# One core: attention value products of two slots at once, reciprocals as a bank fill, and query products two head groups to a bank

## The reference

```
n1 = layernorm(x)
q, k, v = n1 @ wq + bq, ctx @ wk + bk, ctx @ wv + bv
s = (q k^T / sqrt(32)) * mask;  s = -1e9 where s == 0
a = softmax(s) @ v                       # per head
x = x + a @ wo + bo
n2 = layernorm(x)
x = x + real(ifft(fft(n2) @ W)) + bias   # W complex, 512 x 512
```

## Time and profile before

| | |
|---|---|
| median of three runs | 458.8 us |
| span of the profiled execution | 457.1 us |
| PE busy | 442.1 us (97%) |
| DVE busy | 398.0 us (87%) |
| ACT busy | 372.6 us (82%) |
| POOL busy | 359.6 us (79%) |
| chain that ended last: PE | 79% |
| chain that ended last: DVE | 10% |

### The profile page before, as it was taken

How to read it: one execution, slowest core, us unless ns; L and a number is a source line. 1 busy time by engine, 2 the same in 40 slices (tenths; PEclk the granted TensorE clock), 3 DMA queues, 4 the chain that set the end, 5 groups by cost and what they waited for, 6 DMA issues and landing times.

```text
span 457.1 us, 11172 instructions
## 1 busy us (share of the span) xinstructions
PE 442.1 (97%) x3510; PEld 293.3 (64%) x3510; DVE 398.0 (87%) x630; ACT 372.6 (82%) x1434; POOL 359.6 (79%) x540
## 2 busy tenths in 40 slices
PE   6989898999999999999999999999999999999997
PEld 5777686777666666666666666666666666555444
DVE  3797699899999999999999999999999898999443
ACT  3358597789999999898989898989989888899720
POOL 6588744795889899998989898869899685976663
PEclk9999998999999999999999999999999999999999
DMA  8996752332445454545555445445433334330344
GB/s 288 392 368 182 236 195 71 97 86 71 90 92 142 122 147 115 152 110 143 128 134 138 116 107 148 91 114 147 115 96 70 97 74 98 70 93 13 82 104 126
DMA packets 85287, 60.16 MB, mean 132 GB/s; under 512 B 40141, under 2 KB 72813, under 8 KB 84718
## 3 DMA queue, kind: packets, MB, share of 16 engines
q1 hardware_dynamic: 84508, 59.29, 47.3%
q10 hardware_dynamic: 722, 0.17, 0.2%
HBM read 29.33 MB, written 8.39 MB: 83 GB/s over the span
## 4 chain that ended last, share of the span: by engine, by line
PE 79%; DVE 10%; issue 5%; ACT 3%; DMA 1%; ACTq 0%; POOL 0%; DVEq 0%
PE bank L438 32%; PE bank L525 17%; PE bank L582 10%; PE bank L599 6%; PE scores L570 5%; PE bank L443 4%; DVE zs L867 3%; PE bank L595 3%; DVE zs L860 1%; ACT zs L688 1%; DMA bqb<-in_bq 1%; PE scores L443 1%; DVE cn L883 1%; ACT pt L697 1%; DVE x L845 1%
## 5 line engine op out<-in xcount | busy, mean ns | idle before, releaser
L688 ACT ACTIVATE zs<-zs,nbias 128x128 f32<-128x128 f32 x512 | 199.6, 397 | 8.2 <-POOL nbias L1093 7.9
L688 ACT ACTIVATION_READ_ACCUMULATOR zs<-zs,nbias 128x1 f32 x512 | 99.4, 194 | 0.0
L867 DVE SCALAR_TENSOR_TENSOR zs<-zs 128x1024 f32<-128x1024 f32 x64 | 81.3, 1270 | 0.2
L872 DVE TENSOR_REDUCE nmin<-zs 128x8 f32<-128x1024 f32 x64 | 78.1, 1220 | 2.2
L860 DVE TENSOR_TENSOR zs<-scores,ms 128x1024 f32<-128x1024 f32 x64 | 78.0, 1218 | 0.3 <-issue 0.3
L525 PE MATMUL bank<-xth,wqh 128*128 128x256 f16 x256 | 70.9, 277 | 4.0 <-DVE kl L810 2.0
L697 ACT COPY pt<-bank 128x512 f32<-128x512 f32 x128 | 68.4, 586 | 6.7 <-PE bank L582 6.3
L525 PE MATMUL bank<-xtl,wqh 128*128 128x256 f16 x256 | 70.4, 275 | 0.0
L525 PE MATMUL bank<-xth,wql 128*128 128x256 f16 x256 | 70.4, 275 | 0.0
L582 PE MATMUL bank<-ident,zs 128*128 128x128 f32 x512 | 67.5, 275 | 0.7 <-ACT zs L688 0.7
L1053 POOL TENSOR_TENSOR xs<-xs,bob 128x512 f32<-128x512 f32 (+1 forms) x41 | 42.4, 1036 | 24.5 <-DVE zs L867 24.5
(11 more groups left out here) (118 smaller groups left out, 960.1 us busy)
## 6 DMA issues: line engine op xcount, KB each, us to landing
xs<-in_x SPq DMA_DIRECT2D x16, 512.0 KB, 4.2
xtr<-in_xt SPq DMA_DIRECT2D x16, 512.0 KB, 4.4
out<-x SPq DMA_DIRECT2D x31, 256.0 KB, 2.6
qs<-qh SPq DMA_DIRECT2D x120, 64.0 KB
lp<-in_lparts SPq DMA_DIRECT2D x4, 1024.0 KB, 9.0
qs<-ql SPq DMA_DIRECT2D x60, 64.0 KB
ms<-in_mask SPq DMA_DIRECT2D x16, 128.0 KB, 2.6
wqs<-in_wq SPq DMA_DIRECT2D x2, 512.0 KB, 6.8
```

Of the source, the lines that this page charges most:

```text
L688: last = act.activation(z, z, ACT.Exp, bias=nbias[:, s % 4, i:i + 1], scale=-NEG, accum_out=zsum[:, s % 4, i:i + 1])
L867: dve.scalar_tensor_tensor(out=z, in0=z, scalar=0.0, in1=z, op0=ALU.is_equal, op1=ALU.subtract).then_inc(eq_done, 1)
L872: dve.tensor_reduce(nmin[:, s % 4, :], zs[:, s % NZ].rearrange("p t h k -> p (t h) k"), AX.X, ALU.min).then_inc(mn_done, 1)
```

## The change

Slots are taken in pairs m = (2m, 2m+1) for everything behind the exponentials.

- PV for slots 2m and 2m+1 is done at once, as the **first** item of PE in slot 2m+4: eight products that fill the whole bank CX.
- The four transposes of both slots' spread reciprocals are a new fill `R`, late in slot 2m+4, in a G bank. `lo(R)` on DVE only frees the bank, once ACT has copied it.
- Query products of two head groups are one fill `QQ` (24 matmuls into 512 columns), late in odd slots from 7 on (and in slots 2, 4, 5, 6). The mean and deviation rows are a late fill `ST` of their own in slots with r = 0.
- `rec`, `cn`, `ch`, `cl`, reciprocal and spread are one operation for a pair, in odd slots, with twice the columns and one buffer; `qh` and `ql` of a QQ are one operation each.

The core of the diff:

```diff
-    queries = {2: [(2, 0), (2, 1)], 3: [(2, 2)], 4: [(2, 3), (3, 0)], 5: [(3, 1)], 6: [(3, 2), (3, 3)]}
+    queries = {2: (2, 0), 4: (2, 1), 5: (3, 0), 6: (3, 1)}
...
-        late = [("Q",) + f for f in queries.get(v, [divmod(v + 9, 4)]) if f[0] < NC]
+        late = []
+        if v % 2 == 0 and 0 <= v - 4 < NS:
+            late.append(("R", (v - 4) // 2))
+        if v % 4 == 0 and 3 <= v // 4 + 2 < NC:
+            late.append(("ST", v // 4 + 2))
+        if v in queries:
+            late.append(("QQ",) + queries[v])
+        elif v >= 7 and v % 2 == 1 and (v + 9) // 4 < NC:
+            late.append(("QQ", (v + 9) // 4, (v + 9) % 4 // 2))
...
         items = []
+        if v % 2 == 0 and 0 <= v - 4 < NS:
+            items += [("PV", (v - 4) // 2)]
         if 0 <= v - 2 < NS:
             items += [("PT", v - 2, 0), ("PT", v - 2, 1)]
         items += [("G", n) for n in mids]
         if 0 <= v + 1 < NS:
             items += [("S", v + 1, 0), ("S", v + 1, 1)]
-        if 0 <= v - 3 < NS:
-            items += [("PV", v - 3)]
         items += [("G", n) for n in lates]
...
+                elif kind == "QQ":
+
+                    pe.wait_ge(p_l1, c)
+                    for i in range(2):
+                        g = slice(256 * f + 128 * i, 256 * f + 128 * i + 128)
+                        mm = []
+                        for k in range(4):
+                            mm += [(wqh[:, k, g], xth[:, c % 2, k]), (wql[:, k, g], xth[:, c % 2, k]),
+                                   (wqh[:, k, g], xtl[:, c % 2, k])]
+                        last = full_mm(o[:, 256 * i:256 * i + 256], mm)
+                elif kind == "R":
+                    pe.wait_ge(p_rz, c + 1)
+                    for i in range(2):
+                        for t in range(2):
+                            a = 256 * i + 128 * t
+                            last = pe.transpose(o[:, a:a + 128], rzb[:, i, 4 * t:4 * t + 4, :], ident[:])
...
+            def weigh(m):
+                c, h = divmod(m, 2)
                 b = c // (NC // NB)
-                pe.wait_ge(pt_copied, 2 * s + 2)
-                if s >= 1:
-                    pe.wait_ge(cn_done, s)
+                pe.wait_ge(pt_copied, 4 * m + 4)
+                if m >= 1:
+                    pe.wait_ge(cn_done, m)
...
+                for i in range(2):
+                    for j in range(4):
+                        n = 32 * (8 * h + 4 * i + j)
+                        last = pe.matmul(CX[32 * j:32 * j + 32, 256 * i:256 * i + 256], vs[:, b, n:n + 32],
+                                         pt[:, i, j, :], start=True, stop=True)
...
+            def copy_rec(m):
+                n = at["R", m]
+                act.wait_ge(g_done, n + 1)
+                if m >= 1:
+                    act.wait_ge(cn_done, m)
+                act.copy(rec[:], G[n % 3][:].rearrange("p (i n) -> p i n", i=2)).then_inc(rc_done, 1)
...
-                if 0 <= v - 4 < NS:
-                    copy_rec(v - 4)
+                if v % 2 == 1 and 0 <= v - 5 < NS:
+                    copy_rec((v - 5) // 2)
...
+                elif kind == "R":
+                    dve.wait_ge(rc_done, c + 1)
...
-                elif kind == "ST":
+                elif kind in ("ST", "R"):
                     dve.engine_nop().then_inc(g_free, 1)
                     return
...
+            def ctx_norm(m):
+                dve.wait_ge(rc_done, m + 1)
+                if m >= 1:
+                    dve.wait_ge(p_cl, m)
+                dve.tensor_tensor(cn[:], CX[:].rearrange("p (i n) -> p i n", i=2), rec[:], ALU.mult).then_inc(cn_done, 1)
...
-                if v <= VP and 0 <= v - 3 < NS:
-                    spread(v - 3)
+                if v == VP:
+                    spread(0)
...
-                if v >= VP and 0 <= v - 2 < NS:
-                    spread(v - 2)
+                if v > VP and v % 2 == 1 and 0 <= v - 3 < NS:
+                    spread((v - 3) // 2)
```

More of the change, by code:

```diff
@@ L254, in build, with last_query @@
         for n, f in enumerate(fills):
-            if f[0] in ("Q", "U", "M", "K", "W1", "Z"):
+            if f[0] in ("Q", "QQ", "U", "M", "K", "W1", "Z"):
                 hi_count[n] = len(hi_count) + 1
+        def last_query(c):
+            return at["Q", c, 3] if c < 2 else at["QQ", c, 1]
         def tile_of(c, t):
@@ L334, in stack_q @@
             def stack_q(c):
-                sp.wait_ge(g_free, at["Q", c, 3] + 1)
+                sp.wait_ge(g_free, last_query(c) + 1)
                 if c >= 2:
@@ L345, in turn_x1n @@
                 if c == NC - 1:
-                    sp.wait_ge(g_done, at["Q", c, 3] + 1)
+                    sp.wait_ge(g_done, last_query(c) + 1)
                     sp.wait_ge(h2_done, n + 1)
@@ L524, in fill @@
                     for i, (a, b) in enumerate(mm):
[L525 to L531, removed]
+                        pe.matmul(o[:, 0:256], a, b, start=(i == 0), stop=False)
+                    pe.wait_ge(wz_lo, f // 2 + 1)
+                    pe.wait_ge(st_done, c + 1)
+                    last = pe.matmul(o[:, 0:256], wz[:, g], srow[:, c], start=False, stop=True)
+                elif kind == "QQ":
[13 more added lines that the diff above has]
+                            last = pe.transpose(o[:, a:a + 128], rzb[:, i, 4 * t:4 * t + 4, :], ident[:])
                 elif kind == "WO":
                     pe.wait_ge(o_lo, 2)
-                    pe.wait_ge(ch_done, 4 * c + 4)
-                    pe.wait_ge(p_cl, 4 * c + 4)
+                    pe.wait_ge(ch_done, 2 * c + 2)
+                    pe.wait_ge(p_cl, 2 * c + 2)
                     g = slice(128 * f, 128 * f + 128)
@@ L583, in turn @@
                 last.then_inc(pt_done, 1)
-            def weigh(s):
-                c, g = divmod(s, 4)
+            def weigh(m):
+                c, h = divmod(m, 2)
                 b = c // (NC // NB)
-                pe.wait_ge(pt_copied, 2 * s + 2)
-                if s >= 1:
-                    pe.wait_ge(cn_done, s)
+                pe.wait_ge(pt_copied, 4 * m + 4)
+                if m >= 1:
+                    pe.wait_ge(cn_done, m)
                 else:
                     pe.wait_ge(g_free, at["V", 0] + 1)
[L593 to L600, removed]
+                for i in range(2):
[3 more added lines that the diff above has]
+                                         pt[:, i, j, :], start=True, stop=True)
                 last.then_inc(pv_done, 1)
@@ L655, in hi @@
                 elif kind == "Q":
-                    if f == 2 and 3 <= c + 1 < NC:
-                        stat_copy(src, c + 1).then_inc(st_done, 1)
+                    last = act.copy(qh[:, c % 2, f, :], src[:, 0:256])
+                elif kind == "QQ":
                     if f == 0 and c == 2:
@@ L661, in hi @@
                         act.wait_ge(d_q[c % 2], stacked(c - 2))
-                    last = act.copy(qh[:, c % 2, f, :], src[:, 0:256])
+                    last = act.copy(qh[:, c % 2, 2 * f:2 * f + 2, :], src[:].rearrange("p (g n) -> p g n", g=2))
                 last.then_inc(g_hi, 1)
@@ L671, in split_hi @@
                 if c >= 2:
[L672 removed]
+                    act.wait_ge(g_done, last_query(c - 2) + 1)
                 act.copy(xth[:, c % 2], xtr[:, c % NT]).then_inc(h1_done, 1)
@@ L695, in copy_pt, with ctx_hi @@
                 if f == 0 and s >= 2:
-                    act.wait_ge(pv_done, s - 1)
+                    act.wait_ge(pv_done, s // 2)
                 act.copy(pt[:, s % 2, 2 * f:2 * f + 2, :], PB[f][:]).then_inc(pt_copied, 1)
[L699 to L706, removed]
+            def copy_rec(m):
[4 more added lines that the diff above has]
+                act.copy(rec[:], G[n % 3][:].rearrange("p (i n) -> p i n", i=2)).then_inc(rc_done, 1)
+            def ctx_hi(m):
+                c, h = divmod(m, 2)
+                act.wait_ge(cn_done, m + 1)
+                if h == 0 and c >= 2:
                     act.wait_ge(g_done, at["WO", c - 2, 1] + 1)
-                act.copy(ch[:, c % 2, g, :], cn[:, s % 2, :]).then_inc(ch_done, 1)
+                act.copy(ch[:, c % 2, 2 * h:2 * h + 2, :], cn[:]).then_inc(ch_done, 1)
             act.dma_start(bkc[:], bk).then_inc(d_b, 16)
@@ L763, in _ @@
                     exps(v - 1, 1)
-                if 0 <= v - 4 < NS:
-                    ctx_hi(v - 4)
+                if v % 2 == 1 and 0 <= v - 5 < NS:
+                    ctx_hi((v - 5) // 2)
                 if 0 <= v - 9 < 4:
@@ L833, in lo @@
                     last = dve.tensor_tensor(ql[:, c % 2, f, :], src[:, 0:256], qh[:, c % 2, f, :], ALU.subtract)
+                elif kind == "QQ":
+                    g = slice(2 * f, 2 * f + 2)
+                    last = dve.tensor_tensor(ql[:, c % 2, g, :], src[:].rearrange("p (g n) -> p g n", g=2),
+                                             qh[:, c % 2, g, :], ALU.subtract)
                 elif kind == "WO":
@@ L873, in least, with recip @@
```

(29 more changed lines are left out.)

## The result

The changed kernel takes 487.49 us (median of four runs, 486.98 to 487.75) against 458.81 before (458.41 to 458.97): ratio 1.0625, 95% interval 1.0611 to 1.064. It is **slower by 28.7 us**; forecast were 484 us and a range of 468 to 500. Its profiled execution spans 486.0 us.

A forecast was written before the change was run, and what follows sets the result against it. PE was taken to bound the kernel. The profile's 457.1 plus 14.0 (periods), 6.1 (start), 0 (end) and 5 (clock) gave 482.2; with the median 1.7 above the span, 484 us, range 468 to 500.

The forecast's parts named there:

- The added wait: In each slot with r = 1, PE's QQ waits 1.74 us for R's bank, freed behind DVE's minimum.
- the sum: Durations added from an even slot's head (r = 0): `ql` at 4.91, QQ at 11.25, period 25.89; also stepped through the start.
- The periods: Slots 12 to 54: eleven periods of four slots, each 1.27 us longer than 24.62, +14.0 us.
- The start: Slots 4 to 11: U of slot 5 and M of slot 9 wait for R's bank; +6.1 us, 2 to 9.
- my heads: Predicted start times of slots 6 to 12: 74.0, 82.3, 88.1, 95.5, 106.6, 111.3 and 118.4 us.
- The clock: PE falls to half clock once more in the start and in three of eleven periods; +5 us.
- The end: Slots 55 to 63 gain 0.6 us, the last WO comes 0.6 later in the tail; sum zero.
- (a): PE's clock falls in every period, 20.4 us in place of 5: 499 us; chance 0.13.
- (b): QQ's wait is about half, 0.9 us, period +0.4, start +4, no more clock falls: 467.5 us; chance 0.13.
- (c): Faster: R's bank is freed about when PE comes, periods gain 3.5 us, start nothing: 455 us; chance 0.09.
- (d): PV on PE costs 1.78 us a pair as before, +0.2 a pair: 486 us; chance within the main case's 0.62.
- the 1.1 to 1.2 that I gave as a sign: Sign that the forecast is right: PE's PV of eight products takes 1.1 to 1.2 us.

The follow-up runs named there:

- the version with the extra operation ahead of the freeing: Changed kernel plus one idle 1.22 us DVE operation directly ahead of freeing R's bank in slots 13, 17, ... 53; 503.37 us.
- both edits: Changed kernel with R's bank freed right behind `cn` and the eight products moved behind the scores of slot 2m+3; 461.03 us.
- the early freeing alone: Changed kernel with DVE freeing R's bank right behind `cn` instead of behind the minimum; 463.71 us.

## Why the prediction was right

**The added wait, right in place and size.** From the first product of slot 28 (timeline: PT at 229.87, products 1.00 before it, 228.87) to QQ at 240.12 are 11.25 us; the sum said 11.25. That it is exact is luck: two terms missed by 0.11 in opposite directions.

```profile
233.67 0.69 DVE L862 TENSOR_TENSOR ql<-bank,qh 128x512 f16<-128x512 f32 x1
234.28 0.68 DVE L869 SCALAR_TENSOR_TENSOR x<-bank,xs 128x512 f32<-128x512 f32 x1
235.00 0.69 DVE L971 BATCH_NORM_STATS2 st<-x 128x6 f32<-128x512 f32 x1
...
235.83 1.23 DVE L890 TENSOR_TENSOR zs<-scores,ms 128x1024 f32<-128x1024 f32 x1
236.97 0.68 DVE L914 TENSOR_TENSOR cn<-bank,rec 128x512 f32<-128x512 f32 x1
237.57 1.22 DVE L897 SCALAR_TENSOR_TENSOR zs<-zs 128x1024 f32<-128x1024 f32 x1
238.82 1.22 DVE L902 TENSOR_REDUCE nmin<-zs 128x8 f32<-128x1024 f32 x1
```

These are DVE's rows of that stretch, to be read beside the earlier trace rows. `ql` starts 4.80 after the head, not 4.91: eight products in a row take 1.00 us, not 1.14. From `x` to the next mask product are 1.55, not 1.44: taking the reciprocal out saved nothing there, since the aggregate then waits for the statistics before it. `ql` and `cn` cost 0.61 and 0.60, as worked out from 256 columns. PE was ready 9.59 after the head (238.01 + 0.45), not 9.51, so it waited 1.66; the row's 1.50 counts from the modelled end of the last score matmul. The period is 26.02, 0.13 above the sum. That `ql` of the even slot hangs on `qh` held as well, but in slot 28 only by 0.2 us: DVE's own queue was nearly as late, which the sum did not work out.

**The periods, right; +16.8 for +14.0.** The nine periods from slot 16 to slot 52 are 0.16 longer than the sum, 1.4 of the 2.8 in all. Another 0.9 is the first: slot 12 to 16 lasts 27.49 against 25.32 before, since DVE comes out of the start late and ST waits 1.44 for it. The last 0.5 lies in slots 52 and 53: a whole wait, but only half of a period's gain on PE, where I took an eleventh whole period.

**The start, right in cause and too small: +10.8 for +6.1.** The step that was mis-sized is M in slot 9. Up to there my heads held within 0.9 us (PT of slot 7 at 83.01, said 82.3; of slot 9 at 96.03, said 95.5). Then the sum had M start at 101.8 (the head of slot 10 at 106.6, less 4.8 of PE's work). It started at 103.45 and ran at half clock, in the timeline of PE:

```profile
69.83 1.99 PE L454 MATMUL bank<-tb,lp 128*128 128x256 f32 x8 [3.22 <-DVEq L847]
...
103.45 3.78 PE L454 MATMUL bank<-tb,us 128*128 128x256 f32 x8 [3.78 <-DVEq L847]
```

Both are waits for R's bank, U in slot 5 and M in slot 9, as named. In slot 9 `lo(R)` stood behind `ml`, which waited 0.81 for `mh` and then took 1.22, where in the same slot of the kernel before it took 0.69 (97.92); why it took longer was not tried:

```profile
102.15 1.22 DVE L881 SCALAR_TENSOR_TENSOR ml<-mf,mh 128x512 f16<-128x512 f32 x1 [0.81 <-ACT mh L688]
```

The head of slot 12 came at 123.08, 4.7 later than the 118.4 of the sum. Of this 1.65 is M's late start: 0.5 from the head of slot 9, the rest from the wait for `mh` and the longer `ml`. Another 2.7 were lost by the half clock that began while PE waited for M (5.4 us of work at half rate).

**The clock, wrong for the periods.** I had let it fall in three of eleven periods; it fell in none, in a profiled execution with eleven idles of 1.5 us. It fell once in the start, as before, but stayed at half from about 102 to 108.9 us (the window from 108 to 109 has 0.57). PE idled in the first 1.4 us of this, so 2.7 us of work were lost there instead of 1.7: the term is 1.0 where I had 5. It hid, by luck, most of what the start, the periods and the end lacked; without it the sum would have been 479, still inside the range.

**The end, +1.8 for +0.6.** The pair's `cl` takes 1.16 where one slot's took 0.68, and the last WO fills stand behind it; how the rest divides was not tried.

**Rivals.** (a) did not come: no fall in any period. (b) and (c) needed `ql` earlier than the chain allows; it started within 0.11 of where the sum had it, and with `qh` out of the way DVE would have come only 0.2 earlier, so (c) had no ground in this slot. (d): PV was cheaper than before, 1.00 for eight products, and also than the 1.1 to 1.2 that I gave as a sign.

## What to carry to other kernels

In a rotation of buffers that is freed in order, count the fills between producer and waiter again after every edit of the list, and the work of the waiting engine between them: two merges, each of which alone left the period nearly as it was, made nine fills of eight, and one tenant's release came in the very slot that waits for it, behind 4 us of unrelated work. When an engine releases a buffer by an empty instruction, put that instruction where the buffer's last reader is known to be done, not where the list of evacuations happens to stand. And look at what hangs on a producer before moving work ahead of it: PV ahead of PT delayed everything behind PT by 1.00 us, and taking it away shortened the period by 1.19.

## What the runs showed of the hardware

**How long PE idles does not alone decide whether its clock falls.** In the kernel before, the clock fell with an idle of 1.60 us. In the changed kernel it did not fall with 3.22 us in slot 5 and did with 3.78 us in slot 9 (windows: PE busy, clock, DMA share, GB/s):

```profile
71.00:73.00 2.00, 2.00 (x21) 1.00 0.23 55
102.00:104.00 2.00, 0.55 (x1) 0.51 0.00 0
104.00:106.00 2.00, 2.00 (x6) 0.50 0.00 0
```

The list of work does not decide it either. Up to slot 12 the version with the extra operation ahead of the freeing is the changed kernel. Its U of slot 5 waited as long, and it ran at half clock (the window from 68 to 69 us has 0.74, the one from 69 to 70 has 0.50):

```profile
69.66 2.93 PE L456 MATMUL bank<-tb,lp 128*128 128x256 f32 x6 [3.21 <-DVEq L849]
```

In the periods of that version eleven waits of PE for the bank last 2.62 us each; after one of them its clock was half. The timeline shows it in the duration of the first matmul behind the wait, 0.39 for 0.28:

```profile
219.97 0.28 PE L456 MATMUL bank<-xth,wqh 128*128 128x256 f16 x1 [2.62 <-DVEq L849]
...
328.56 0.39 PE L456 MATMUL bank<-xth,wqh 128*128 128x256 f16 x1 [2.62 <-DVEq L849]
```

and the windows of that version the clock (same columns as above):

```profile
326.00:328.00 2.00, 0.00 (x0) 0.97 0.69 206
328.00:330.00 2.00, 1.45 (x7) 0.50 0.84 241
330.00:332.00 2.00, 2.00 (x15) 0.67 0.12 49
```

Two idles of the same length, 2.62 us, with and without a fall. What else decides was not tried.

**The falls set runs of one kernel apart.** With both edits the runs at a mean granted clock of 1.000 took 460.3 to 461.29 us, those at 0.996 took 462.34 and 462.85; with the early freeing alone it was 462.48 and 463.69 to 463.8. A mean of 0.996 is about what one stretch of 3.4 us at half leaves over such a span (1.7 of 462 us). Versions that differ by less than 1 to 2 us can be told apart only by runs of the same mean clock.

**A row of products 32 columns wide pays something at its ends.** Four took 0.57 us, eight 1.00, from the first start to the next instruction; and the group ahead of them is longer by about 0.1 than where other work follows it, 0.32 for 0.22 in the two transposes and 0.54 for 0.45 in the scores (with both edits). So eight cost 1.10 between two other shapes and four 0.67, not half of it.

**Doubling the columns of a DVE operation on 256** cost 0.26 to 0.27 us, in `cn` (0.41 to 0.68) and `ql` (0.42 to 0.69).
